# Pair attention on one core: one product for four pairs through widened queries and values

## The chip, the cores and the metric

One core of a Trainium2 chip runs the whole program. The time is the device time of one execution in microseconds; the reference for it is the median of three executions. A profiled execution is a separate one, and its rows give the durations used below. PE is TensorE, DVE is VectorE, ACT is ScalarE, POOL is GpSimd, SP issues the DMAs; PEld stands for TensorE's weight loads.

## What is computed

The program is a small Perceiver of six stages on a state x of 64 batches, 32 tokens and 128 features (2048 tokens). The change lies in the fifth stage, whose reference is, cut to what matters:

```python
x = x + attn(layernorm(x), Wq, Wk, Wv)        # b, s, d = 64, 32, 128; H = 16, dk = 8

Q = (x @ Wq.T).reshape(H, b, s, dk)           # a plain reshape, K and V the same way
scores = einsum('hbqd,hbkd->hbqk', Q, K)
out = einsum('hbqk,hbkd->hbqd', softmax(scores, -1), V).reshape(b, s, -1)
y = out + x
(y - mean(y, axis=(1, 2))) / sqrt(var(y, axis=(1, 2)) + 1e-5)
```

The reshape doesn't split heads by feature: 32 rows of one "head and batch" are two tokens in a row with their 16 slices of 8 features. So attention runs within pairs of neighbouring tokens: 1024 pairs, each with a 32x32 score matrix and 8 features of depth.

## The kernel before

All is float32. The state lies with features on partitions, [128, 2048]. `perceiver` runs the stages one after the other with a barrier between them; `l1_attention` (from L1345) is the stage in question. Within it each engine has its own program in order, and semaphores tie them together.

Front: mean and variance over features by products with a constant matrix (L1499, L1503), normalised x in `xn`; projections q, k, v in four parts of 512 tokens (`project`, L1509), copied out of PSUM by ScalarE (`keep`, L1591, q and v) and VectorE (k, L1708). A DMA stores each part in DRAM (L1437), another reads it back by head (`by_heads`, L1442): group g (512 tokens) lies on partitions 32g to 32g+32, of which every fourth holds one of the 8 features; the other 24 stay zero, for which GpSimd clears the three tiles first (L1489). The free axis is [16 slices, 512 tokens].

Block loop: eight blocks of 32 pairs in each of the four groups, 128 pairs and 1024 columns a block. GpSimd reorders q into a row per pair (`q_st`, L1494). `scores(i)` on TensorE makes 128 products, each of 32 rows, 32 columns and 32 moving columns, on one of the four diagonal 32x32 tiles of the array; `turns` orders them so that neighbours in time lie in different groups. VectorE's `softmax(i)`: maximum (L1658), subtraction (L1661), then the exponential on ScalarE (L1595), sum (L1663), reciprocal (L1665), product (L1667), transpose of each 32x32 block (L1670). `turn_v` copies and transposes the values of the next block (L1650, L1653). `outputs(i)` makes 128 products of the same form (L1532), and ScalarE's `keep_output` copies the result into `o8` (L1599), which is the q tile. Scores have two PSUM buffers, outputs one. TensorE's order is scores(0), scores(1), outputs(0), scores(2), outputs(1) and so on.

Each two blocks complete 128 tokens of every group, a chunk of 512 tokens: SP stores them (L1470) and reads them back with features on partitions (L1484); VectorE adds the residual (L1680), and sums over 16 batches at a time lead to the centred, scaled result added to x (L1682 to L1698), with TensorE's L1538 and L1543 and ScalarE's L1603, L1608, L1610 in between. The last chunk's chain ends the stage.

Other lines named below: L2746 (products of the fourth stage, 128x128 loads, 32 moving columns), L1863 and L1899 (first stage), L1114 (the router of the sixth stage, 128x128 loads, 8 moving columns).

Of the kernel before, what the change touches and what calls it, by code (L numbers as in the profile page):

```python
# [6 lines left out]
P = 128  # L7
B, S, D = 64, 32, 128
TOK = B * S
# [3 lines left out]
F32 = mybir.dt.float32  # L13
# [1330 lines left out]

def l1_attention(nc, x_in, consts, dram):  # L1345
# [3 lines left out]
    with ExitStack() as ctx:  # L1349
        def sb(name, shape, dt=F32):  # L1350
# [4 lines left out]
        ones, eps5 = consts["mean"], consts["eps5"]  # L1355
        ps = ctx.enter_context(nc.psum_tensor("t_ps", [P, 8 * BANK], F32))
        scratch = [nc.dram_tensor(f"t_scratch{i}", (P, TOK), F32, kind="Internal").ap() for i in range(4)]
# [4 lines left out]
        by_head = [sb(n + "8", [P, HEADS, GTOK]) for n in "qkv"]  # L1362
        q_st = sb("qs", [P, 2, BCOL])
        v_st = sb("vs", [P, BCOL])
        v_rows = sb("v_rows", [P, 2, BCOL])
# [4 lines left out]
        o8, o_t, square = by_head[0], tmp, q_t  # L1370
# [4 lines left out]
        w_loaded, cleared = sem("w_loaded"), sem("cleared")  # L1375
        projected, kept, spread = ([sem(what + n) for n in "qkv"] for what in ("projected_", "kept_", "spread_"))
        stored = [[sem(f"stored_{n}{p}") for p in range(4)] for n in "qkv"]
        q_staged, v_staged, v_turned, scored, maxed, shifted, exped, summed, inverted, scaled, p_turned, attended, o_kept = (
            sem(n) for n in ("q_staged", "v_staged", "v_turned", "scored", "maxed", "shifted", "exped", "summed",
                             "inverted", "scaled", "p_turned", "attended", "o_kept"))  # L1380
        o_stored = sem("o_stored")
# [13 lines left out]

        out_ps = ps[:, 4 * BANK:4 * BANK + BCOL]
# [5 lines left out]
        def heads_of(ap, i):  # L1402

            return ap[:, :, i * 2 * BPAIRS:(i + 1) * 2 * BPAIRS].rearrange("p j (n t) -> p n j t", t=2)
# [4 lines left out]
        def turns():  # L1409

            for s in range(BPAIRS):
                for g in range(GROUPS):
                    yield g, (s + g * BPAIRS // GROUPS) % BPAIRS

        def chunk(ap, c):

            return ap[:, :].rearrange("p (g t) -> p g t", g=GROUPS)[:, :, c * P:(c + 1) * P]

        def packed(ap, c):

            return ap[:, of(c)].rearrange("p (g t) -> p g t", g=GROUPS)

        def rows_in(g):
            return slice(32 * g, 32 * (g + 1), ROW_STEP)

        def in_scratch(i, g, first, last):

            return scratch[i].rearrange("(j c) t -> c j t", c=DH)[:, :, g * GTOK + first:g * GTOK + last]

        with nc.Block() as block:  # L1430
            @block.sync
            def _(sp):
                sp.dma_start(wqkv[:, :, :], dram["attn1"]).then_inc(w_loaded, 16)

                def store(i, p):
                    sp.wait_ge(kept[i], p + 1)
                    sp.dma_start(scratch[i][:, of(p)], qkv_t[i][:, of(p)]).then_inc(stored[i][p], 16)  # L1437

                def by_heads(i, p):
                    sp.wait_ge(stored[i][p], 16)  # L1440
                    sp.wait_ge(cleared, i + 1)
                    sp.dma_start(by_head[i][rows_in(p), :, :], in_scratch(i, p, 0, GTOK)).then_inc(spread[i], 16)  # L1442

                store(0, 0)
                store(0, 1)
                store(1, 0)
                by_heads(0, 0)
                store(0, 2)
                store(1, 1)
                by_heads(0, 1)  # L1450
                by_heads(1, 0)
                store(0, 3)
                store(1, 2)
                by_heads(0, 2)
                by_heads(1, 1)
                store(1, 3)
                by_heads(0, 3)
                store(2, 0)
                by_heads(1, 2)
                store(2, 1)  # L1460
                by_heads(1, 3)
                store(2, 2)
                by_heads(2, 0)
                store(2, 3)
                for p in range(1, 4):
                    by_heads(2, p)

                def store_output(first, last):
                    for g in range(GROUPS):
                        sp.dma_start(in_scratch(3, g, first, last), o8[rows_in(g), :, first:last]).then_inc(o_stored, 16)  # L1470

                stores = 0
                for c in range(CHUNKS):
                    if c < CHUNKS - 1:
                        sp.wait_ge(o_kept, 2 * c + 2)
                        store_output(c * P, (c + 1) * P)
                        stores += GROUPS
                    else:
                        for h in range(2):
                            sp.wait_ge(o_kept, 2 * c + 1 + h)  # L1480
                            store_output(c * P + h * (P // 2), c * P + (h + 1) * (P // 2))
                            stores += GROUPS
                    sp.wait_ge(o_stored, 16 * stores)
                    sp.dma_start(packed(o_t, c), chunk(scratch[3], c)).then_inc(o_loaded[c], 16)  # L1484
# [12 lines left out]
            def _(pe):  # L1497
# [7 lines left out]
                def project(i, p):  # L1505
# [3 lines left out]
                    nc.tensor.matmul(bank(4 + p if i == 1 else p), wqkv[:, i, :], xn[:, of(p)],  # L1509
                                     start=True, stop=True).then_inc(projected[i], 1)  # L1510
# [1578 lines left out]
```

## Time and profile before

| | |
|---|---|
| median of 3 executions | 2837.02 us (2836.5 to 2841.46) |
| profiled execution | 2837.81 us, span 2835.7 us |
| mean granted TensorE clock | 0.925 |
| PE / PEld busy | 2469.1 us (87%) / 1394.8 us (49%) |
| DVE / ACT / POOL busy | 2181.6 us (77%) / 1854.4 us (65%) / 841.8 us (30%) |
| pair attention | about 2410 to 2576 us of the span |
| L1522 + L1532 (its products), recorded busy | 32.6 + 32.8 us |

Busy is the time in which an engine has at least one instruction recorded; matmuls are pipelined, so the mean length of one (237 ns for L1522) is latency and not its share of the time: that is read from how many lie in a stretch. Granted clock 1.00 is 2.4 GHz, 0.50 is 1.2 GHz. "Issue" is time in which an engine waited for nothing that the profile shows. The shares are over all six stages; what a change in one is worth is read from that stage's own windows.

### The profile page before, as it was taken

To read this page: it belongs to the slowest core of one execution; us is meant where nothing else is said; L and a number is where in the kernel's file an instruction comes from. 1 tells how busy PE (TensorE), PEld (TensorE's weight loads), DVE (VectorE), ACT (ScalarE), POOL (GpSimd) and SP (SyncE) were. 2 spreads that over 40 slices of the span, in tenths; PEclk is the share of its full clock that TensorE was granted. 3 is DMA by queue.
4 is the path that set the end of the run, shared out by engine and by line. 5 is a ranking of instruction groups with operands and counts; after the bars stand their busy time and mean duration, and the time that the engine had idled before them with its cause. 6 is when DMAs were issued, how large, how long until landed. Compare 5 with 4: busy or idle time off the path is not lost. (4 is left out here: it accounts for less than half of the span.)

```text
span 2835.7 us, 35494 instructions
## 1 busy us (share of the span) xinstructions
PE 2469.1 (87%) x12324; PEld 1394.8 (49%) x12350; DVE 2181.6 (77%) x2846; ACT 1854.4 (65%) x2597; POOL 841.8 (30%) x470
## 2 busy tenths in 40 slices
PE   6799999998799999999999999998446887556997
PEld 3466666663344444444444444443124776354775
DVE  5687777772999999999999999996557776465554
ACT  5465555554799888888889988886425664214443
POOL 0121211111444444444444444443001000301554
PEclk9999999999999999999999999999657999656999
DMA  1000000002000000000000000000000110200221
GB/s 69 12 19 16 17 18 16 15 1 82 0 0 0 38 0 38 0 37 0 38 0 23 14 0 38 0 0 0 12 21 15 37 37 15 94 27 25 76 69 38
DMA packets 26069, 68.11 MB, mean 24 GB/s; under 512 B 3192, under 2 KB 15288, under 8 KB 24632
## 3 DMA queue, kind: packets, MB, share of 16 engines
q1 hardware_dynamic: 25632, 64.13, 6.6%
q8 instruction: 81, 1.33, 0.2%
q10 hardware_dynamic: 288, 2.10, 0.2%
q14 instruction: 68, 0.56, 0.1%
HBM read 60.91 MB, written 5.31 MB: 23 GB/s over the span
## 5 line engine op out<-in xcount | busy, mean ns | idle before, releaser
L251 PE MATMUL a_ps<-a_x,a_w 128*128 128x512 f32 x1536 | 695.9, 598 | 25.8 <-DVE a_kf L599 13.2
L251 PEld LDWEIGHTS a_ps<-a_x,a_w 128*128 128x128 f32 x1536 | 291.6, 191 | 405.5 <-issue 368.0
L774 POOL TENSOR_TENSOR a_den<-a_qf,a_ksum 128x1024 f32<-128x1024 f32 x128 | 271.0, 2117 | 512.4 <-DVE a_qf L592 475.8
L777 POOL TENSOR_TENSOR a_num<-a_qf,a_kvsum 128x1024 f32<-128x1024 f32 x128 | 294.8, 2303 | 185.6 <-DVE a_kvsum L617 185.6
L2425 DVE TENSOR_REDUCE x_rn<-x_sqk 128x8 f32<-128x512 f32 x256 | 174.3, 682 | 106.4 <-ACT x_sqk L2349 102.3
L2349 ACT ACTIVATE x_sqk<-x_b_k 128x512 f32<-128x512 f32 x256 | 153.1, 598 | 157.2 <-PE x_b_k L2261 150.9
L262 PE MATMUL a_ps<-a_att,a_w 128*128 128x512 f32 x480 | 215.8, 592 | 0.0
L592 DVE SCALAR_TENSOR_TENSOR a_qf<-a_eq,a_qf 128x1024 f32<-128x1024 f32 x128 | 195.4, 1527 | 1.7
L2242 POOL TENSOR_TENSOR x_kn<-x_craw,x_w 128x256 f32<-128x256 f32 x64 | 46.9, 734 | 503.8 <-DVE x_craw L2414 482.2
L445 ACT ACTIVATE a_den<-a_den,consts 128x1024 f32<-128x1024 f32 x128 | 147.0, 1149 | 55.9 <-POOL a_den L774 55.9
L599 DVE SCALAR_TENSOR_TENSOR a_kf<-a_ek,a_ps 128x1024 f32<-128x1024 f32 x128 | 155.6, 1215 | 30.2 <-ACT a_ps L441 22.8
L611 DVE SCALAR_TENSOR_TENSOR a_ek<-a_ps,a_w,a_kf 128x1024 f32<-128x1024 f32 x128 | 163.2, 1275 | 9.9 <-PE a_ps L251 9.8
L440 ACT ACTIVATE a_ek<-a_ps,a_w 128x1024 f32<-128x1024 f32 x128 | 142.2, 1111 | 36.5 <-PE a_ps L251 30.5
L2261 PE MATMUL x_b_k<-x_wk_hi,x_kt_hi 128*128 128x512 f32 x256 | 160.2, 626 | 4.7 <-DVE x_kt_lo L2420 4.7
L624 DVE SCALAR_TENSOR_TENSOR a_att<-a_num,a_den 128x1024 f32<-128x1024 f32 x128 | 155.7, 1217 | 5.4 <-ACT a_den L447 4.3
L433 ACT ACTIVATE a_eq<-a_ps,a_w 128x1024 f32<-128x1024 f32 x128 | 142.1, 1110 | 24.4 <-PE a_ps L251 16.7
L605 DVE TENSOR_REDUCE a_ksum<-a_kf 128x32 f32<-128x1024 f32 x128 | 155.2, 1212 | 1.1
L617 DVE TENSOR_REDUCE a_kvsum<-a_ek 128x32 f32<-128x1024 f32 x128 | 155.3, 1213 | 0.6
L1229 POOL TENSOR_TENSOR m_hid_lo<-m_hid,m_hid_hi 128x1024 fp32r<-128x1024 f32 (+1 forms) x48 | 118.1, 2462 | 118.1 <-ACT m_hid_hi L1197 117.7
L262 PEld LDWEIGHTS a_ps<-a_att,a_w 128*128 128x128 f32 x480 | 91.2, 190 | 114.8 <-issue 114.8
L434 ACT ACTIVATE a_qf<-a_ps,a_w 128x1024 f32<-128x1024 f32 x128 | 142.4, 1113 | 0.0
L2275 PE MATMUL x_b_y<-x_sc,x_kn 128*128 128x512 f32 x256 | 140.4, 633 | 0.5 <-DVE x_sc L2435 0.5
(398 smaller groups left out, 5307.9 us busy)
## 6 DMA issues: line engine op xcount, KB each, us to landing
a_w<-layers SPq DMA_DIRECT2D x8, 2577.0 KB, 9.4
x_craw<-ctx SPq DMA_DIRECT2D x32, 256.0 KB, 2.7
y_cx<-ctx_t SPq DMA_DIRECT2D x16, 512.0 KB, 3.6
m_wb<-m_scratch SPq DMA_DIRECT2D x16, 512.0 KB, 3.8
m_w<-experts SPq DMA_DIRECT2D x8, 544.0 KB, 4.9
x_w<-xattn_w ACTq DMA_DIRECT2D x1, 1536.0 KB, 9.4
x_all<-x_t SPq DMA_DIRECT2D x4, 256.0 KB, 9.3
t_scratch<-t_q_t SPq DMA_DIRECT2D x4, 256.0 KB, 3.7
```

The costliest lines, as they stand in the source:

```text
L251: last = nc.tensor.matmul(bank(tile, j), col(par, part * HK + u * P, P), x[:, t0:t0 + BANK], start=True, stop=True)
L262: last = nc.tensor.matmul(bank(tile_t, j), col(par, C_WO + c * D, D), bank(att[:, half, c, :], j), start=(c == 0), stop=(c == CH - 1))
L592: nc.vector.scalar_tensor_tensor(out=qf[:, b, :], in0=eq[:, b, :], scalar=1.0, in1=qf[:, b, :], op0=ALU.add, op1=ALU.add).then_inc(q_feat, 1)
L599: nc.vector.scalar_tensor_tensor(out=kf[:, b, :], in0=ek[:, b, :], scalar=1.0, in1=tile_k[:, :], op0=ALU.min, op1=ALU.add).then_inc(k_feat, 1)
L605: nc.vector.tensor_reduce(ksum[:, b, :], by_batch(kf[:, b, :]), AX_X, ALU.add).then_inc(k_summed, 1)
L611: nc.vector.scalar_tensor_tensor(out=ek[:, b, :], in0=tile_v[:, :], scalar=bias(par, C_BV + u), in1=kf[:, b, :], op0=ALU.add, op1=ALU.mult ...
L617: nc.vector.tensor_reduce(kvsum[:, b, :], by_batch(ek[:, b, :]), AX_X, ALU.add).then_inc(kv_summed, 1)
L624: nc.vector.scalar_tensor_tensor(out=att[:, half, c, :], in0=num[:, b, :], scalar=1.0, in1=den[:, b, :], op0=ALU.mult, op1=ALU.mult).then_ ...
L774: nc.gpsimd.tensor_tensor(by_batch(den[:, b, :]), by_batch(qf[:, b, :]), bcast(ksum[:, b, :], S), ALU.mult).then_inc(d_ready, 1)
L777: nc.gpsimd.tensor_tensor(by_batch(num[:, b, :]), by_batch(qf[:, b, :]), bcast(kvsum[:, b, :], S), ALU.mult).then_inc(n_ready, 1)
L2261: last = nc.tensor.matmul(b_k[n % 2][:, :], a[:, b % 4, t], k[:, f], start=(p == 0), stop=(p == 2))
L2425: nc.vector.tensor_reduce(rn[:, b % 4, 8 * c:8 * c + 8], sqk[:, n % 2, :].rearrange("p (h d) -> p h d", d=XDH), AX_X, ALU.add).then_inc(n_ ...
```

## The change

The queries lie on all 32 partitions of a group: feature c of token part p (four parts of 128 tokens) on partition 4c + p. A group of 512 tokens is now worked through in two blocks of 64 tokens of each part (block i: group i // 2, half i % 2), so that a block still has 128 pairs and 1024 columns. For each of the block's 32 places, four pairs (one of each part) share the same 32 partitions. `q_st` becomes four copies of the queries side by side, in copy p all partitions but those of part p multiplied by zero (`wide`; mask `own_row`): three copies by ScalarE (`widen`), the fourth by GpSimd. One product with 32 rows, 128 columns and 32 moving columns then gives the scores of four pairs on 128 partitions, 32 products a block. The values are turned once for all groups (`turn_v`, 2048 columns); `own_values(g)` on ScalarE spreads group g's into `v_own` by four masked copies of 512 elements, so that one product with 128 rows, 32 columns and 32 moving columns gives four pairs' outputs. The probabilities' softmax and transpose stay as they are. There is a tile `o8` of its own, no memsets, one store a block and one load a group (now plain 512 tokens), loads and stores go through new DRAM layouts (runs of 512 B and 2 KB; the output's stores 256 B), and each group's q and k have their own semaphores. The projections' order changes: v's part p follows q's closely, in the same bank. The constants get the two masks.

```diff
 
 
+NPART = 4
+PTOK = GTOK // NPART
+NPAIR = PTOK // 2
+NB = BCOL // PAIR_ROWS
...
+        O_SCRATCH = 2
         xn = sb("xn", [P, TOK])
         tmp = sb("tmp", [P, TOK])
         wqkv = sb("wqkv", [P, 3, P])
...
+        q_st = sb("qs", [P, 2, NPART * NB * PAIR_ROWS])
+        v_st = sb("vs", [P, NPAIR * PAIR_ROWS])
+        v_rows = sb("v_rows", [P, NPAIR * PAIR_ROWS])
+        v_own = sb("v_own", [P, 2, NPAIR * PAIR_ROWS])
         prob = sb("prob", [P, BCOL])
         prob_t = sb("prob_t", [P, 2, BCOL])
-        red = sb("red", [P, BPAIRS])
+        red = sb("red", [P, NB])
...
             sem(n) for n in ("mean_ready", "centred", "squared", "var_ready", "logged", "rstd_ready", "normed"))
-        w_loaded, cleared = sem("w_loaded"), sem("cleared")
...
+        def wide(i, p):
+
+            return q_st[group_rows(i // 2), i % 2, :].rearrange("r (n a j t) -> r n a j t", a=NPART, j=HEADS, t=2)[:, :, p, :, :]
+
+        def group_rows(g):
+            return slice(32 * g, 32 * (g + 1))
+
+        def by_row(i, g):
+
+            return scratch[i][g].rearrange("j r t -> r j t")
+
+        def by_feature(i, g):
+
+            return scratch[i][g].rearrange("j (c p) t -> (j c) (p t)", c=DH)
+
+        def values_by_row(p):
+            return v_scratch[:, :, p, :].rearrange("j r t -> r j t")
+
+        def values_by_feature(g):
+            return v_scratch.rearrange("j (c g) p t -> (j c) g (p t)", c=DH)[:, g, :]
 
...
+                    sp.dma_start(values_by_feature(p) if i == 2 else by_feature(i, p), qkv_t[i][:, of(p)]).then_inc(stored[i][p], 16)
+
+                def by_heads(i, g):
+                    sp.wait_ge(stored[i][g], 16)
+                    sp.dma_start(by_head[i][group_rows(g), :, :], by_row(i, g)).then_inc(spread[i][g], 16)
+
+                def values_by_part(p):
+                    for g in range(GROUPS):
+                        sp.wait_ge(stored[2][g], 16)
+                    sp.dma_start(v8[group_rows(p), :, :], values_by_row(p)).then_inc(v_spread, 16)
 
...
                 store(0, 0)
+                store(1, 0)
+                store(2, 0)
+                store(2, 1)
+                by_heads(0, 0)
+                by_heads(1, 0)
+                store(2, 2)
...
+                store(1, 1)
+                for p in range(NPART):
+                    values_by_part(p)
+                by_heads(0, 1)
+                by_heads(1, 1)
...
+                for g in range(2, GROUPS):
+                    by_heads(0, g)
+                    by_heads(1, g)
+
+                for i in range(BLOCKS):
+                    g, h = i // 2, i % 2
+                    t = slice(h * (PTOK // 2), (h + 1) * (PTOK // 2))
+                    sp.wait_ge(o_kept, i + 1)
+                    sp.dma_start(by_row(O_SCRATCH, g)[:, :, t], o8[group_rows(g), :, t]).then_inc(o_stored[g], 16)
+                    if h == 1:
+                        sp.wait_ge(o_stored[g], 32)
+                        sp.dma_start(o_t[:, of(g)], by_feature(O_SCRATCH, g)).then_inc(o_loaded[g], 16)
 
             @block.gpsimd
             def _(pool):
-                for t in by_head:
-                    nc.gpsimd.memset(t[:, :, :], 0.0).then_inc(cleared, 1)
                 for i in range(BLOCKS):
-                    if i == 0:
-                        pool.wait_ge(spread[0], 16 * GROUPS)
-                    wait_past(pool, scored, i - 1)
-                    nc.gpsimd.tensor_copy(rows_of(q_st[:, i % 2, :]), heads_of(by_head[0], i)).then_inc(q_staged, 1)
+                    if i % 2 == 0:
+                        pool.wait_ge(spread[0][i // 2], 16)
+                    r, p = group_rows(i // 2), NPART - 1
+                    nc.gpsimd.tensor_scalar(wide(i, p), by_pair(q8[r, :, :], i % 2 * NB, (i % 2 + 1) * NB), own_row[r, p:p + 1], None,
+                                            ALU.mult).then_inc(q_masked, 1)
 
...
                 def scores(i):
-                    pe.wait_ge(q_staged, i + 1)
-                    if i == 0:
-                        pe.wait_ge(spread[1], 16 * GROUPS)
+                    g, h = i // 2, i % 2
+                    pe.wait_ge(q_widened, (NPART - 1) * (i + 1))
+                    pe.wait_ge(q_masked, i + 1)
+                    pe.wait_ge(spread[1][g], 16)
                     wait_past(pe, shifted, i - 1)
...
-                    out = scores_of(i)
-                    for g, n in turns():
-                        c = slice(n * PAIR_ROWS, (n + 1) * PAIR_ROWS)
-                        r = slice(32 * g, 32 * g + 32)
-                        t = 2 * (i * BPAIRS + n)
-                        last = nc.tensor.matmul(out[r, c], q_st[r, i % 2, c], by_head[1][r, :, t:t + 2], start=True, stop=True)
+                    out, r = scores_of(i), group_rows(g)
+                    for n in range(NB):
+                        t = 2 * (h * NB + n)
+                        last = nc.tensor.matmul(out[:, n * PAIR_ROWS:(n + 1) * PAIR_ROWS], q_st[r, h, n * P:(n + 1) * P], k8[r, :, t:t + 2],
+                                                start=True, stop=True)
                     last.then_inc(scored, 1)
 
                 def outputs(i):
-                    pe.wait_ge(v_turned, i + 1)
+                    g, h = i // 2, i % 2
+                    pe.wait_ge(v_masked, NPART * (g + 1))
                     pe.wait_ge(p_turned, i + 1)
                     wait_past(pe, o_kept, i)
-                    for g, n in turns():
+                    for n in range(NB):
                         c = slice(n * PAIR_ROWS, (n + 1) * PAIR_ROWS)
-                        r = slice(32 * g, 32 * g + 32)
-                        last = nc.tensor.matmul(out_ps[r, c], v_rows[r, i % 2, c], prob_t[r, i % 2, c], start=True, stop=True)
+                        v = slice((h * NB + n) * PAIR_ROWS, (h * NB + n + 1) * PAIR_ROWS)
+                        last = nc.tensor.matmul(out_ps[group_rows(g), c], v_own[:, g % 2, v], prob_t[:, i % 2, c], start=True, stop=True)
                     last.then_inc(attended, 1)
...
                 project(0, 0)
+                project(1, 0)
+                project(2, 0)
                 project(0, 1)
-                project(1, 0)
-                project(0, 2)
+                project(2, 1)
                 project(1, 1)
-                project(0, 3)
-                project(1, 2)
-                project(1, 3)
-                for p in range(4):
+                for p in range(2, 4):
+                    project(0, p)
                     project(2, p)
+                    project(1, p)
...
+                def widen(i):
+                    if i % 2 == 0:
+                        act.wait_ge(spread[0][i // 2], 16)
+                    r = group_rows(i // 2)
+                    for p in range(NPART - 1):
+                        nc.scalar.activation(wide(i, p), by_pair(q8[r, :, :], i % 2 * NB, (i % 2 + 1) * NB), ACT.Copy,
+                                             scale=own_row[r, p:p + 1]).then_inc(q_widened, 1)
+
+                def own_values(g):
+                    act.wait_ge(v_turned, 1)
+                    wait_past(act, attended, 2 * (g - 1))
+                    turned = v_rows[:, :].rearrange("k (n c g) -> k n c g", g=GROUPS, c=DH)
+                    dst = v_own[:, g % 2, :].rearrange("k (n c a) -> k n c a", a=NPART, c=DH)
+                    for p in range(NPART):
+                        nc.scalar.activation(dst[:, :, :, p], turned[:, :, :, g], ACT.Copy, scale=own_group[:, p:p + 1]).then_inc(v_masked, 1)
+
                 def keep_output(i):
+                    r = group_rows(i // 2)
                     act.wait_ge(attended, i + 1)
-                    nc.scalar.activation(heads_of(o8, i), rows_of(out_ps), ACT.Copy).then_inc(o_kept, 1)
+                    nc.scalar.activation(by_pair(o8[r, :, :], i % 2 * NB, (i % 2 + 1) * NB), rows_of(out_ps[r, :]), ACT.Copy).then_inc(o_kept, 1)
 
                 def squares(c):
...
                 exponentials(0)
-                for i in range(1, 5):
-                    exponentials(i)
-                    keep_output(i - 1)
+                widen(2)
+                exponentials(1)
+                own_values(0)
+                keep_output(0)
+                exponentials(2)
+                widen(3)
+                keep_output(1)
+                own_values(1)
+                exponentials(3)
+                widen(4)
+                keep_output(2)
+                exponentials(4)
...
                 keep_output(4)
...
+                own_values(3)
...
-                def turn_v(i):
-                    if i == 0:
-                        dve.wait_ge(spread[2], 16 * GROUPS)
-                    wait_past(dve, v_turned, i)
-                    nc.vector.tensor_copy(rows_of(v_st[:, :]), heads_of(by_head[2], i)).then_inc(v_staged, 1)
-                    dve.wait_ge(v_staged, i + 1)
-                    wait_past(dve, attended, i - 1)
-                    nc.vector.transpose(v_rows[:, i % 2, :], v_st[:, :]).then_inc(v_turned, 1)
+                def turn_v():
+                    dve.wait_ge(v_spread, 16 * NPART)
+                    nc.vector.tensor_copy(rows_of(v_st[:, :]), by_pair(v8, 0, NPAIR)).then_inc(v_staged, 1)
+                    dve.wait_ge(v_staged, 1)
...
+                    if i == 0:
+                        turn_v()
                     if i == 3:
                         add_residual(0)
                     if i == 4:
...
+    for a in range(4):
+        c[:, 264 + a] = np.arange(P) % 4 == a
+        c[:, 268 + a] = np.arange(P) // 32 == a
```

## Rows read from the trace of the kernel before

**Rows 1.** Windows of this stage: us, then each engine's busy time, PEclk, DMA.
```profile
core 0: us, PE busy (x) PEld busy (x) DVE busy (x) ACT busy (x) POOL busy (x), PEclk, DMA share, GB/s
2428.80:2441.50 12.70, 0.00 (x0) 0.00 (x0) 0.00 (x0) 0.00 (x0) 3.97 (x3) 0.68 0.66 247
2441.50:2560.70 119.20, 63.97 (x4103) 59.60 (x4103) 74.16 (x78) 17.77 (x19) 6.34 (x6) 0.50 0.10 29
```
**Rows 2.** Groups of instructions by form, 2404 to 2592 us: busy, mean, idle before.
```profile
line engine op names shapes xcount | busy us, mean ns | idle before us <-releasers
L1532 PE MATMUL t_ps<-t_prob_t,t_v_rows 32*32 32x32 f32 x2048 | 32.8, 237 | 29.3 <-issue 23.9 <-DVE t_prob_t L1670 4.0 <-ACT t_q L1599 1.3
L1522 PE MATMUL t_ps<-t_k,t_qs 32*32 32x32 f32 x2048 | 32.6, 237 | 39.3 <-issue 25.9 <-DMA t_k<-t_scratch 13.4
...
L1653 DVE STREAM_TRANSPOSE t_v_rows<-t_vs 128x1024 f32<-128x1024 f32 x8 | 10.0, 1245 | 0.3
...
L1599 ACT ACTIVATE t_q<-t_ps 128x1024 f32<-128x1024 f32 x8 | 8.6, 1076 | 30.7 <-PE t_ps L1532 30.7
L1595 ACT ACTIVATE t_prob<-t_prob 128x1024 f32<-128x1024 f32 x8 | 8.5, 1056 | 72.1 <-DVE t_prob L1661 72.1
L1494 POOL COPY t_qs<-t_q 128x1024 f32<-128x1024 f32 x8 | 8.4, 1055 | 78.2 <-PE t_ps L1522 71.4 <-DMA t_q<-t_scratch 6.9
...
L1650 DVE COPY t_vs<-t_v 128x1024 f32<-128x1024 f32 x8 | 5.3, 659 | 23.0 <-DMA t_v<-t_scratch 23.0
```
**Rows 3.** Timeline of blocks 3 and 7: start, length, then idle time before.
```profile
2481.53 1.93 PE L1522 MATMUL t_ps<-t_k,t_qs 32*32 32x32 f32 x128 [1.96 <-issue]
...
2486.84 1.22 DVE L1658 TENSOR_REDUCE t_red<-t_ps 128x32 f32<-128x1024 f32 x1 [6.17 <-PE t_ps L1522]
...
2489.36 1.06 ACT L1595 ACTIVATE t_prob<-t_prob 128x1024 f32<-128x1024 f32 x1 [9.34 <-DVE t_prob L1661]
...
2493.35 1.25 DVE L1670 STREAM_TRANSPOSE t_prob_t<-t_prob 128x1024 f32<-128x1024 f32 x1
...
2545.62 1.23 DVE L1658 TENSOR_REDUCE t_red<-t_ps 128x32 f32<-128x1024 f32 x1 [3.41 <-PE t_ps L1522]
```
**Rows 4.** Timeline of the front of the stage: memset, last copy, first product.
```profile
2423.82 6.92 POOL L1489 MEMSET t_v<- 128x8192 f32 x1
...
2428.18 0.60 ACT L1591 ACTIVATE t_v_t<-t_ps 128x512 f32<-128x512 f32 x1 [0.26 <-PE t_ps L1509]
...
2441.55 2.67 PE L1522 MATMUL t_ps<-t_k,t_qs 32*32 32x32 f32 x183 [13.41 <-DMA t_k<-t_scratch]
```
**Rows 5.** Timeline, weight loads alone: the first load after a wait, four forms.
```profile
2399.98 0.19 PEld L2746 LDWEIGHTS y_ps<-y_qt,y_kvm 128*128 128x128 f32 x1 [1.17 <-DVE y_qk L2956]
...
87.22 0.11 PEld L1899 LDWEIGHTS x_pa<-x_wvo,x_kn_cols 128*32 128x32 f32 x1 [0.17 <-issue]
...
2501.70 0.29 PEld L1538 LDWEIGHTS t_ps<-t_sums,consts 128*128 128x128 f32 x1
...
2441.52 0.12 PEld L1522 LDWEIGHTS t_ps<-t_k,t_qs 32*32 32x32 f32 x1 [14.21 <-issue]
```
**Rows 6.** Timeline of three streams of loads; window of the first one's clock.
```profile
2591.05 3.11 PEld L1114 LDWEIGHTS m_ps<-m_router,m_xn 128*128 128x128 f32 x14
...
2399.98 0.97 PEld L2746 LDWEIGHTS y_ps<-y_qt,y_kvm 128*128 128x128 f32 x8 [1.17 <-DVE y_qk L2956]
...
24.15 1.86 PEld L1863 LDWEIGHTS x_pa<-x_w 64*128 64x128 f32 x16 [1.60 <-issue]
...
2591.00:2594.80 3.80, 3.80 (x20) 3.80 (x19) 1.63 (x2) 1.26 (x3) 0.00 (x0) 0.50 0.00 0
```
**Rows 7.** The page's DMA issues: count, KB each, median us to landing.
```profile
t_scratch<-t_q_t SPq DMA_DIRECT2D x4, 256.0 KB, 3.7
```
**Rows 8.** Timeline of the end of the stage, from the last output copy on.
```profile
2560.78 1.04 ACT L1599 ACTIVATE t_q<-t_ps 128x1024 f32<-128x1024 f32 x1 [6.48 <-PE t_ps L1532]
...
2567.85 0.69 DVE L1698 TENSOR_TENSOR x_all<-x_all,t_tmp 128x512 f32<-128x512 f32 x1
2568.92 0.69 DVE L1680 TENSOR_TENSOR t_tmp<-t_tmp,t_xn 128x512 f32<-128x512 f32 x1 [0.38 <-DMA t_tmp<-t_scratch]
...
2575.30 0.69 DVE L1698 TENSOR_TENSOR x_all<-x_all,t_tmp 128x512 f32<-128x512 f32 x1
```

More of the change, by code:

```diff
@@ L1353, in l1_attention @@
         sem = ctx.enter_context(semaphores(nc, "t_"))
-        ones, eps5 = consts["mean"], consts["eps5"]
+        ones, eps5, own_row, own_group = consts["mean"], consts["eps5"], consts["own_row"], consts["own_group"]
         ps = ctx.enter_context(nc.psum_tensor("t_ps", [P, 8 * BANK], F32))
-        scratch = [nc.dram_tensor(f"t_scratch{i}", (P, TOK), F32, kind="Internal").ap() for i in range(4)]
+        scratch = [[nc.dram_tensor(f"t_scratch{i}{g}", (HEADS, DH * NPART, PTOK), F32, kind="Internal").ap() for g in range(GROUPS)]
+                   for i in range(3)]
+        v_scratch = nc.dram_tensor("t_v_scratch", (HEADS, DH * GROUPS, NPART, PTOK), F32, kind="Internal").ap()
+        O_SCRATCH = 2
         xn = sb("xn", [P, TOK])
@@ L1394, in scores_of, with project_bank @@
             return ps[:, i % 2 * BCOL:(i % 2 + 1) * BCOL]
+        def project_bank(i, p):
+            return bank(4 + p if i == 1 else p)
         out_ps = ps[:, 4 * BANK:4 * BANK + BCOL]
@@ L1400, in pairs, with by_pair @@
             return ap.rearrange("p (n r) -> p n r", r=PAIR_ROWS)
-        def heads_of(ap, i):
-            return ap[:, :, i * 2 * BPAIRS:(i + 1) * 2 * BPAIRS].rearrange("p j (n t) -> p n j t", t=2)
+        def by_pair(ap, first, last):
+            return ap[:, :, 2 * first:2 * last].rearrange("p j (n t) -> p n j t", t=2)
         def rows_of(ap):
             return ap.rearrange("p (n j t) -> p n j t", j=HEADS, t=2)
[L1409 to L1428, printed above, removed]
+        def wide(i, p):
[10 more added lines that the diff above has]
+            return v_scratch.rearrange("j (c g) p t -> (j c) g (p t)", c=DH)[:, g, :]
         with nc.Block() as block:
@@ L1452, in _ @@
                 store(0, 3)
-                store(1, 2)
-                by_heads(0, 2)
-                by_heads(1, 1)
                 store(1, 3)
[L1457 to L1484, printed above, removed]
+                for g in range(2, GROUPS):
+                    by_heads(0, g)
+                    by_heads(1, g)
@@ L1508, in project @@
                         pe.wait_ge(kept[0], p + 1)
-                    nc.tensor.matmul(bank(4 + p if i == 1 else p), wqkv[:, i, :], xn[:, of(p)],
+                    nc.tensor.matmul(project_bank(i, p), wqkv[:, i, :], xn[:, of(p)],
                                      start=True, stop=True).then_inc(projected[i], 1)
                 def scores(i):
-                    pe.wait_ge(q_staged, i + 1)
-                    if i == 0:
-                        pe.wait_ge(spread[1], 16 * GROUPS)
+                    g, h = i // 2, i % 2
@@ L1590, in keep @@
                     act.wait_ge(projected[i], p + 1)
-                    nc.scalar.activation(qkv_t[i][:, of(p)], bank(p), ACT.Copy).then_inc(kept[i], 1)
+                    nc.scalar.activation(qkv_t[i][:, of(p)], project_bank(i, p), ACT.Copy).then_inc(kept[i], 1)
                 def exponentials(i):
@@ L1620, in _ @@
                     nc.scalar.activation(tmp[:, of(p)], tmp[:, of(p)], ACT.Exp, scale=-0.5).then_inc(rstd_ready, 1)
-                for i in (0, 2):
-                    for p in range(4):
-                        keep(i, p)
-                exponentials(0)
-                for i in range(1, 5):
-                    exponentials(i)
-                    keep_output(i - 1)
+                for p in range(4):
+                    keep(0, p)
+                    keep(2, p)
+                widen(0)
+                widen(1)
+                exponentials(0)
+                widen(2)
[10 more added lines that the diff above has]
+                exponentials(4)
+                widen(5)
+                keep_output(3)
+                own_values(2)
                 squares(0)
                 exponentials(5)
+                widen(6)
                 keep_output(4)
@@ L1632, in _ @@
                 exponentials(6)
+                widen(7)
                 keep_output(5)
+                own_values(3)
                 squares(1)
@@ L1697, in finish @@
                     dve.wait_ge(y_normed, c + 1)
-                    nc.vector.tensor_tensor(chunk(x_in, c), chunk(x_in, c), packed(o_t, c), ALU.add).then_inc(out_done, 1)
+                    nc.vector.tensor_tensor(x_in[:, of(c)], x_in[:, of(c)], o_t[:, of(c)], ALU.add).then_inc(out_done, 1)
                 for p in range(4):
@@ L3029, in consts_of @@
     return {"mean": c[:, 0:128], "ident": c[:, 128:256], "eps5": c[:, 256:257], "eps6": c[:, 257:258],
-            "ln256": c[:, 258:259], "eps10": c[:, 259:260], "all": c[:, :]}
+            "ln256": c[:, 258:259], "eps10": c[:, 259:260], "own_row": c[:, 264:268],
+            "own_group": c[:, 268:272], "all": c[:, :]}
 def pack_layers(a):
```

37 lines of the change are left out of this document (14 added, 23 removed).

## The prediction

> **What bounds the kernel now.** The span is a row of stages separated by barriers, and the change touches one of them, the pair attention, which runs from about 2410 to 2576.0 us. So I read by stage: first the windows over the block loop, then the groups of this stage, then one block in the timeline. In the loop (2441.5 to 2560.7, 119.2 us) TensorE is recorded busy 64.0 us and VectorE 74.2 us, and neither looks full; the granted clock is 0.50 all through, so TensorE is at 1.2 GHz [rows 1]. The reader is to see that the busy shares mislead. Each block has 128 score products and 128 output products, and the trace has 2048 matmul records for the 1024 products of either kind, so a product is two passes [rows 2]. A batch of 128 passes takes 1.93 us and then the engine stands 1.96 us on "issue" [rows 3]: it waits for its own instructions. Two batches for scores and two for outputs make 4 x 3.9 = 15.6 us at most; the start of the softmax moves from 2486.84 to 2545.62 in four blocks, 14.7 us each [rows 3]. The softmax itself, from the first reduction at 2486.84 to the end of the transpose (2493.35 + 1.25), is 7.76 us, so VectorE waits for TensorE in each block. The bound is the number of TensorE instructions.
>
> **What is removed.** A block now has 32 + 32 products instead of 128 + 128: 64 passes for scores and 64 for outputs. The issue stalls end; at the present pace (128 passes in 3.9 us) 64 would need 2.0 us, and the work on the array will be longer than that. The memsets go: the third ended at 2423.82 + 6.92 = 2430.7, 10.8 us before the first product, which waited for the load of k [rows 4], so this is worth nothing by itself. Seven of eight value turns leave VectorE, where it waits anyway.
>
> **What a score product costs now.** This is the term that decides. Each product loads 128 columns of widened queries (32 rows deep) and streams only 32 columns of keys. The stage has only loads of 32x32, so I take the load from elsewhere, by the first load after a wait, which has nothing in front of it. At the high clock 128x128 takes 0.19 us and 128x32 takes 0.11 [rows 5]: 96 columns more cost 0.08, 0.83 ns a column. At the low clock 128x128 takes 0.29 and 32x32 takes 0.12 [rows 5]: 0.17 for 96 columns, which is the doubled rate (0.16) although the second is 32 rows deep. So the load goes by columns, the rows give nothing back, and 128 columns cost 107 ns at the high and 213 ns at the low clock.
> Streams confirm it: 14 loads of 128 columns before products with 8 moving columns take 3.11 us at clock 0.50, (3.11 - 0.33)/13 = 0.214 us each, and at the high clock 8 loads before 32 moving columns take 0.97, (0.97 - 0.19)/7 = 0.111 [rows 6]. The 32 moving columns are hidden under the next load, on the same rows; so too with 64 rows, 16 in 1.86 us, 0.111 each, where load and stream are both 128 columns [rows 6].
> Now the clock. In the loop it is low already. Of the new stream the nearest row is the one of the router: TensorE busy 3.80 of 3.80 us with loads of 128 columns and short moving sides, and the clock stays at 0.50 [rows 6]. I take the low clock. Scores of a block: 63 x 0.213 + 0.07 + 0.37 for the last product = 13.9 us, against about 7.8 now. Bounds: 0.111 a pass (high clock, 7.3 us) and 0.267 (load and stream one after the other, 17.3 us).
>
> **What an output product costs.** 128 rows, 32 columns to load, 32 to stream: 53 ns each at the low clock. Today four row groups work side by side and 128 passes take 1.93 us, (1.93 - 0.24)/127 x 4 = 53 ns for each group [rows 2, 3], so load and stream overlap: 64 x 0.053 + 0.2 = 3.6 us; bounds 1.9 (high clock) and 7.0 (one after the other).
>
> **What is added on ScalarE, and who waits.** widen(i) is three activations of 1024 elements a partition, 1.06 us each by the exponential and the strided output copy [rows 2]: 3.24 us a block; own_values(g) is four of 512 elements, 4 x (0.60 + 0.05) = 2.6 us [rows 4]. They are 32 partitions wide, which I don't count as cheaper. From block 3 on the order on ScalarE is exponentials(i), widen(i+1). The exponential needs scores(i), and scores(i+1) needs widen(i+1). So the two score buffers no longer let TensorE run ahead; each block is a ring: scores 13.9, then to VectorE and through reduction and subtraction 0.09 + 1.26 + 1.26, exponential to its end 1.06, widening 3.27, back to TensorE 0.07: 13.9 + 7.0 = 20.9 us. (2489.36 - 2486.84 = 2.52 is the start of the exponential after the start of the softmax [rows 3].) Outputs (3.6), the output copy and own_values lie beside it, as does the rest of the softmax; GpSimd's masking of the fourth part (1.06 us by its copy of q [rows 2]) waits for its load only.
>
> **The sum.** Start: today the last copy of the projections ends at 2428.8 [rows 4]. In the new order each projection of v waits for the copy of q of its part in the same bank, 0.6 + 0.2 us four times, and the last copy ends at about 2431.8. The q and k loads of group 0 are issued by 2427 and stores of this size land in 3.7 us [rows 7], so they are there. widen(0) ends at 2435.1; the first scores start at 2435.2, 6.3 us earlier than today's 2441.55 [rows 4]. Bounds for this start: 2433 and 2438.
> First blocks: scores(0) and scores(1) end at 2463.0. VectorE has finished softmax(0) and the one turn of all values (twice 0.66 + 1.25 [rows 2], 3.85 us) by 2460.8, under cover of scores(1). exponentials(1) ends 3.6 later, own_values(0), queued behind it, 2.6 after that, and outputs(0) waits for both: 3.6, then scores(2) 13.9. The softmax of block 2 starts at 2486.7.
> Blocks 3 to 7: 5 x 20.9 = 104.5, so softmax(7) starts at 2591.2, against 2545.62.
> End: softmax 7.8, outputs(7) 3.6, copy 1.1. Today the copy ends at 2561.82, the last chunk's first addition is at 2568.92 and the stage ends at 2575.99 [rows 8]. The new store is one issue instead of four, but VectorE finishes chunk 2 only at 2568.54 [rows 8], a chain behind the same copy, so 13.8 of today's 14.2 us stay. The stage ends at 2591.2 + 26.3 = 2617.5, which is 41.5 us later. The clock fell today some 5 us after the last projection (mean 0.68 over 2428.8 to 2441.5 [rows 1]: 4.6 us at 1.00); the new scores begin 3 us after it, so some 16 passes run at the high level and give back 1.7 us. 39.8 more.
> The profiled execution took 2837.81 us (span 2835.7), 0.8 over the median of 2837.02. 2837.8 + 39.8 = 2877.6, predicted as 2878. Its own range: start +-3, ring +-0.4 five times, outputs serial twice (+7), high clock through scores(0) (-7): 2866 to 2890.
>
> **Rivals.**
> Fast, high clock (faster): the longer products keep TensorE at 2.4 GHz. With 7.3 and 1.9 us: 2435.2 + 7.3 + 11.6 (now VectorE's softmax(0) and turn) + 3.6 + 2.6 + 1.9 + 7.3 = 2469.5; + 5 x 14.3 = 2541.0; + 24.6 = 2565.6, 10.4 us earlier, 2827. For it: TensorE would be busy for 17.5 of 20.9 us in the forecast, where now it is 64.0 of 119.2 [rows 1]. Against it: the router's rows. The point from which the sign turns is a score stage of 8.3 us, that is 0.130 us a pass, since the time is 2517.9 + 7 x stage while the stage is under 11.6.
> Fast, cheap load (faster): 128 columns load in 107 ns at the low clock too when only 32 rows are filled: scores 7.1, 2470.8 + 5 x 14.1 + 26.3 = 2567.6, 8.4 earlier, 2829. Against it: 0.12 for 32x32 fits the column rate without any discount.
> The Trainium skill, page "TensorE: Matmul & The Clock Gate", section "LDWEIGHTS (loading the stationary operand)", gives columns / 1.2 ns whatever the rows, an estimate of 107 ns; by it the sum would be this rival's. The trace has that for fp32 only at the high clock and twice it (0.214) at the low one.
> Serial (slower still): load and stream don't overlap within one group of 32 rows: passes of 0.267 and 0.107, stages of 17.3 and 7.0: 2435.2 + 3 x 17.3 + 6.2 + 7.0 = 2500.3, + 5 x 24.3 + 29.7 = 2651.5, 75.5 later, 2913. Against it: the 64-row stream at 0.111.
> The same page, section "Part 3: Packing small matmuls — row/col tiling", says that a load overlaps running products only where the row group differs; by that rule this rival is the forecast. The trace disagrees for the full array and for 64 rows, and has no 32-row tile with one group alone.
> Issue-bound as the change supposes (products nearly free) would need passes of about 30 ns; the load rows exclude it.
>
> **How the numbers follow.** Forecast 0.79; high clock 0.07; cheap load 0.06; serial 0.06; something near no change 0.02. So slower 0.85, faster 0.13, within 0.2% 0.02; 0.2% is 5.7 us, about what a measurement of this kernel can tell from none. The range takes the forecast's own, 2 us of slack below, and the serial case above: 2864 to 2914, 0.82.
>
> **What would show it.** In the profile after: score products 64 records a block with loads about 0.33 us long and 0.213 apart; clock 0.50 over the loop; softmax starts 20.9 us apart, VectorE's first reduction waiting for TensorE some 13 us each time; TensorE waiting for ScalarE's widening about 3.4 us a block; no long waits on issue. Wrong if the passes are 0.11 apart, or if the blocks come at under 15 us.

## The result, and the profile after

| | before | after |
|---|---|---|
| median (range), us | 2837.71 (2836.5 to 2841.46) | 2878.54 (2877.65 to 2880.17) |
| profiled span, us | 2835.7 | 2878.4 |
| pair attention, first mean product to last addition, us | 165.9 | 204.1 |
| before it / behind it in the span, us | 2410.1 / 259.7 | 2412.1 / 262.2 |

The ratio is 1.0142 (95% interval 1.0125 to 1.0160): slower by 40.8 us, where 2878 was predicted. The spans differ by 42.7 us: 38.3 in the changed stage, 1.9 ahead of it and 2.5 behind it. These two lie in work that the change does not touch: over the ten kernels profiled in this study the stage begins between 2407.8 and 2412.1 us, with the same work ahead, and what follows it takes 257.6 to 262.8.

The groups of the block loop in the kernel after (columns as in [rows 2], 2437.7 to 2602.4 us):
```profile
L1529 PE MATMUL t_ps<-t_k,t_qs 32*128 32x32 f32 x512 | 105.5, 384 | 19.3 <-ACT t_qs L1611 19.3
...
L1541 PE MATMUL t_ps<-t_prob_t,t_v_own 128*32 128x32 f32 x512 | 28.4, 239 | 12.4 <-ACT t_v_own L1620 8.1 <-DVE t_prob_t L1710 4.3
...
L1611 ACT ACTIVATE t_qs<-t_q,consts 32x1024 f32<-32x1024 f32 x21 | 23.1, 1160 | 0.1
L1620 ACT ACTIVATE t_v_own<-t_v_rows,consts 128x512 f32<-128x512 f32 x16 | 18.0, 1213 | 0.1
L1501 POOL TENSOR_SCALAR t_qs<-t_q,consts 32x1024 f32<-32x1024 f32 x6 | 17.5, 2922 | 8.7 <-DMA t_q<-t_scratch 8.3
...
L1698 DVE TENSOR_REDUCE t_red<-t_ps 128x32 f32<-128x1024 f32 x8 | 9.8, 1225 | 90.7 <-PE t_ps L1529 90.7
```
TensorE has a quarter of the passes (512 where [rows 2] had 2048) and the wait "issue", 23.9 and 25.9 us there, is gone; yet the score passes are busy 105.5 us instead of 32.6, and the reduction that opens the softmax waits 90.7 us for them, in all eight blocks.

One full block of the timeline, after (start, length, idle time before):
```profile
2507.69 1.22 DVE L1698 TENSOR_REDUCE t_red<-t_ps 128x32 f32<-128x1024 f32 x1 [13.10 <-PE t_ps L1529]
...
2510.21 1.06 ACT L1604 ACTIVATE t_prob<-t_prob 128x1024 f32<-128x1024 f32 x1 [10.86 <-DVE t_prob L1701]
2511.29 3.30 ACT L1611 ACTIVATE t_qs<-t_q,consts 32x1024 f32<-32x1024 f32 x3
...
2514.64 13.86 PE L1529 MATMUL t_ps<-t_k,t_qs 32*128 32x32 f32 x64 [3.77 <-ACT t_qs L1611]
...
2528.53 1.23 DVE L1698 TENSOR_REDUCE t_red<-t_ps 128x32 f32<-128x1024 f32 x1 [11.80 <-PE t_ps L1529]
```
This is the ring: reduction at 2507.69, exponential, three widenings behind it, 64 passes (32 products) in 13.86 us, and the next reduction 20.84 us after the last one. In [rows 3] the softmax started every 14.7 us.

The clock, in windows of the same kernel (columns as in [rows 1]):
```profile
2437.70:2602.40 164.70, 135.93 (x1034) 134.40 (x1034) 63.16 (x64) 59.00 (x58) 17.53 (x6) 0.54 0.15 33
...
2528.50:2549.40 20.90, 18.00 (x132) 17.77 (x133) 7.26 (x9) 10.38 (x10) 0.00 (x0) 0.50 0.07 20
```
Low nearly throughout, though TensorE is busy for 135.9 of 164.7 us.

### The profile page after: what moved, and what is told of

Its sections match the earlier page's. It is cut to its first block and busy times, and to the rows that moved or that the text cites. A ratio compares the mean times of both kernels' runs of the same rounds, so it can differ in the third digit from the quotient of the medians.

```text
span 2878.4 us, 29362 instructions
## 1 busy us (share of the span) xinstructions
PE 2545.3 (88%) x9252; PEld 1472.2 (51%) x9278; DVE 2169.9 (75%) x2832; ACT 1898.1 (66%) x2637; POOL 836.3 (29%) x467
```

## The experiments

Eight kernels, each beside the kernel before. Where a row of the trace answers, it decides; whole times add what moves outside the stage. The kernel before took 2837.74 us beside four of them (the widening moved, the half load, the longer moving side, the outputs alone) and 2841.78 beside the other four, on another chip; each ratio is to the one beside it.

**The ring.** Here ScalarE widens the queries of block i+1 ahead of exponentials(i), from block 2 on.
```diff
-exponentials(2)
 widen(3)
+exponentials(2)
 keep_output(1)
```
(and so for widen(4) to widen(7))

> The changed kernel with one thing moved on ScalarE: widen(i+1) stands ahead of exponentials(i) from block 2 on. Theory (a ring through ScalarE): the score stage of the next block no longer waits for exponential and widening, so the softmax starts come at TensorE's own pace, 64 score passes of 0.213 plus 64 output passes of 0.053, about 17.2 us apart instead of 20.8; five such steps give 18 us, about 2860 us, and the waits of TensorE for the widening (19.3 us in all) nearly vanish. Rival (TensorE's work alone sets the pace, the waits are filled by it anyway): no change, 2878 us.

Measured 2855.39 us, ratio 1.0062 (1.0040 to 1.0083). The start of a block, as above:
```profile
2503.07 3.62 PE L1541 MATMUL t_ps<-t_prob_t,t_v_own 128*32 128x32 f32 x64
2503.18 1.23 DVE L1698 TENSOR_REDUCE t_red<-t_ps 128x32 f32<-128x1024 f32 x1 [9.59 <-PE t_ps L1529]
...
2506.62 13.86 PE L1529 MATMUL t_ps<-t_k,t_qs 32*128 32x32 f32 x64
...
2520.52 1.23 DVE L1698 TENSOR_REDUCE t_red<-t_ps 128x32 f32<-128x1024 f32 x1 [8.29 <-PE t_ps L1529]
```
Steps of 17.34 us: the products of the next block begin straight behind the outputs, and 3.62 + 13.86 = 17.48 of TensorE's own work is now the step. The widening behind the exponential was worth 3.5 us a block. The profiled stage takes 187.2 us instead of 204.1, 17 us less; the median is 23 us below that of the changed kernel, and what exceeds 17 lies outside the stage or between executions (this profile is of the slowest of five, 2861.75 us). Even without it the kernel stays slower than before: its score stage alone nearly fills an old block.

**The price by columns.** Each score product loads 64 of the 128 weight columns; the scores of the other two pairs of each product are not computed.
```diff
-nc.tensor.matmul(out[:, n * PAIR_ROWS:(n + 1) * PAIR_ROWS], q_st[r, h, n * P:(n + 1) * P], k8[r, :, t:t + 2],
+nc.tensor.matmul(out[0:64, n * PAIR_ROWS:(n + 1) * PAIR_ROWS], q_st[r, h, n * P:n * P + 64], k8[r, :, t:t + 2],
```


> The changed kernel with the load of each score product cut from 128 to 64 columns: two of the four pairs are left out (their rows keep old values), so its output is not the reference's. Theory (a score pass costs its weight columns, 1.67 ns each at the low clock): passes of 0.107, score stages of 7.1 instead of 13.9 us, blocks about 14.0 us apart instead of 20.8; 34 us over five blocks and about 10 before them, about 2834 us. Rival (a pass of this form has a fixed price whatever it loads): 2878 us.

Measured 2826.90 us, ratio 0.9964 (0.9952 to 0.9977).
```profile
2493.87 7.03 PE L1529 MATMUL t_ps<-t_k,t_qs 32*64 32x32 f32 x64 [3.43 <-ACT t_qs L1611]
...
2500.94 1.23 DVE L1698 TENSOR_REDUCE t_red<-t_ps 128x32 f32<-128x1024 f32 x1 [4.97 <-PE t_ps L1529]
```
Half the columns take half the time (7.03 against 13.86 us for 64 passes), at the same count of instructions and the same 32 moving columns. Steps fell to 14.0, and some passes ran at the higher clock (two of the stages take 6.40 and 6.49 us). So neither the count nor the moving side sets this stage.

**Longer moving side.** The changed kernel with 128 moving columns for each score product (the keys four times over; each column of the result is written again by its own product later).
```diff
-last = nc.tensor.matmul(out[:, n * PAIR_ROWS:(n + 1) * PAIR_ROWS], q_st[r, h, n * P:(n + 1) * P], k8[r, :, t:t + 2],
+m = min(4, 16 - n % 16)
+moving = k8[r, :, t:t + 2].unsqueeze(1).broadcast_to([32, m, HEADS, 2])
+last = nc.tensor.matmul(out[:, n * PAIR_ROWS:(n + m) * PAIR_ROWS], q_st[r, h, n * P:(n + 1) * P], moving,
```

> The changed kernel, each score product with up to 128 moving columns instead of 32: the same 32 key columns repeated four times, the surplus columns of the result being overwritten by the next products, so the result stays the same and TensorE does up to four times the streaming. Theory (load-bound at the low clock; the clock is low because the array mostly stands while weights load): the pass stays at 0.213 us at the low clock, since 128 columns load as long as 128 stream, but the granted clock rises to 1.00 in the score stages and the pass falls to about 0.11; blocks 14 to 15 us apart, about 2840 us. Rival A (clock stays at 0.50): unchanged within a few us, 2878 to 2882. Rival B (load and stream don't overlap on one group of 32 rows): passes of 0.43, over 2950 us.

Measured 2877.61 us, ratio 1.0138 (1.0112 to 1.0164).
```profile
2437.00:2600.00 163.00, 132.17 (x1016) 130.63 (x1014) 64.72 (x68) 56.55 (x56) 17.63 (x6) 0.55 0.13 30
...
2510.36 13.86 PE L1531 MATMUL t_ps<-t_k,t_qs 32*128 32x128 f32 x64 [3.65 <-ACT t_qs L1613]
```
Four times the streaming cost nothing: 13.86 us again, clock 0.55. I had expected the clock to rise, and was wrong. What it does show is that within one group of 32 rows a load of 128 columns and a stream of 128 columns lie fully side by side, which excludes the serial rival: by it this kernel's 64 passes would take some 27 us (an estimate, 0.213 us for the load and as much for the stream) and the changed kernel's 17.3. The Trainium skill, page "TensorE: Matmul & The Clock Gate", section "Part 3: Packing small matmuls — row/col tiling", has two statements: a load is pulled ahead where the row group differs or where it goes to the background weight buffer, and, below, it overlaps running products only where the row group differs. This trace disagrees with the second.

**All rows.** Two kernels whose score products use all 128 rows (rows of other groups' queries and keys are added in, so their scores are not the reference's), one with 32, one with 128 moving columns. Both wait for all loads of k and for cleared query buffers, and their first product starts 16.6 us late, counted from the start of the stage.
```diff
-nc.tensor.matmul(out[:, n * PAIR_ROWS:(n + 1) * PAIR_ROWS], q_st[r, h, n * P:(n + 1) * P], k8[r, :, t:t + 2],
+moving = k8[:, :, t:t + 2].unsqueeze(1).broadcast_to([P, m, HEADS, 2])
+nc.tensor.matmul(out[:, n * PAIR_ROWS:(n + m) * PAIR_ROWS], q_st[:, h, n * P:(n + 1) * P], moving,
```
(m is 1 in the first, and as in the kernel above in the second)

> The kernel before this one with 32 moving columns again: score products on all 128 rows (not the reference's scores), 128 weight columns, 32 moving. If rows fill time in a load, a pass takes longer than the 0.213 us of 32 rows; if a load goes by columns alone, 64 passes take 13.9 us at clock 0.50 as before, steps of 20.8, and the time is that of the changed kernel and the late start, about 2883. If full rows raise the clock, 7.3 us and 2835.

> The changed kernel with every score product on all 128 rows (the queries and keys of the other three groups are streamed too, so the scores are not the reference's, where those rows aren't zero) and 128 moving columns. It waits for all loads of k and for two cleared query buffers first, so the first block starts up to 6 us later. Rival A with a filled array (the clock would rise, if the array had more to do): 64 passes in 7.3 us, softmax steps of 14.3 us, about 2835 with the late start. My theory after the run with 128 moving columns (that stream stayed at 0.50; the router's stream with full loads too): 13.9 us, steps of 20.8, about 2883. I take the second with 0.6.

Measured 2891.53 and 2867.68 us (one time each, beside 2841.78 for the kernel before on that chip). The first, with 32 moving columns, then the second, with 128, and two of its windows:
```profile
2508.61 13.86 PE L1538 MATMUL t_ps<-t_k,t_qs 128*128 128x32 f32 x64 [3.80 <-ACT t_qs L1622]
```
```profile
2484.44 7.33 PE L1538 MATMUL t_ps<-t_k,t_qs 128*128 128x128 f32 x64
...
2498.77 10.06 PE L1538 MATMUL t_ps<-t_k,t_qs 128*128 128x128 f32 x64 [4.84 <-ACT t_qs L1622]
...
2498.80:2504.00 5.20, 5.20 (x24) 5.20 (x25) 0.77 (x1) 5.17 (x5) 0.00 (x0) 0.50 0.27 75
2504.00:2508.80 4.80, 4.80 (x43) 4.76 (x42) 0.00 (x0) 0.36 (x1) 0.00 (x0) 0.95 0.00 0
```
Rows are free in a load: 128 rows take the 13.86 us of 32; this kernel's stage is 17.9 us longer than the changed one's, nearly all of it the late start. With all rows and 128 moving columns the granted clock did rise during the stream, from 0.50 to 0.95, and the 64 passes took 10.06 us, or 7.33 where the clock was 1.00 from the start: the figure the prediction gave for that rival (7.3). I had taken the low clock for this kernel with 0.6, and missed; its steps, 17.06 us, lie between both expectations and are the ring again, 10.06 + 7.0. So the high-clock rival named a real mechanism, and the change doesn't reach it. Neither the rows alone (the first of these kernels) nor the moving columns alone (the kernel above) did.

**own_values earlier.** own_values(0) ahead of exponentials(1):
```diff
-exponentials(1)
 own_values(0)
+exponentials(1)
```


> The changed kernel with own_values(0) ahead of exponentials(1) on ScalarE. In the changed kernel the four value activations stood behind that exponential and ended at 2472.5 us; outputs(0) waited 8.1 us for them. Theory (that wait is on the path through blocks 0 to 2, and my sum had it too short): they now run from about 2461.7, end at 2466.2, before exponentials(1) is due at 2467.0; outputs(0) starts 6.2 us earlier, and the time falls by 4 to 6 us, to about 2873. The steps of blocks 3 to 7 stay at 20.8 us. If it is the score products of block 2 alone that set the start of softmax 2, nothing moves: 2878.

Measured 2870.58 us, ratio 1.0100 (1.0083 to 1.0117).
```profile
2459.44 4.50 ACT L1620 ACTIVATE t_v_own<-t_v_rows,consts 128x512 f32<-128x512 f32 x4 [4.39 <-DVE t_v_rows L1693]
...
2463.99 3.42 PE L1541 MATMUL t_ps<-t_prob_t,t_v_own 128*32 128x32 f32 x64 [2.23 <-ACT t_v_own L1620]
```
outputs(0) starts 54.5 us into the stage instead of 60.4, and the stage takes 198.9 us instead of 204.1: 5.2 less, with unchanged steps of 20.84. The span fell by 12.2; the other 7 lie outside the stage (2.6 ahead of it, 4.4 behind).

**Outputs alone by four.** The kernel before, with its scores unchanged (32x32, four groups side by side). v of group p goes to partitions 32p + 4c + p instead of 32p + 4c, and one product of 128 rows serves four pairs.
```diff
-sp.dma_start(by_head[i][rows_in(p), :, :], in_scratch(i, p, 0, GTOK)).then_inc(spread[i], 16)
+rows = slice(33 * p, 32 * (p + 1), ROW_STEP) if i == 2 else rows_in(p)
+sp.dma_start(by_head[i][rows, :, :], in_scratch(i, p, 0, GTOK)).then_inc(spread[i], 16)
...
-for g, n in turns():
+for n in range(BPAIRS):
     c = slice(n * PAIR_ROWS, (n + 1) * PAIR_ROWS)
-    last = nc.tensor.matmul(out_ps[r, c], v_rows[r, i % 2, c], prob_t[r, i % 2, c], start=True, stop=True)
+    last = nc.tensor.matmul(out_ps[0:32, c], v_rows[:, i % 2, c], prob_t[:, i % 2, c], start=True, stop=True)
```
The output copy and the stores of o8 follow: 32 partitions, one group on every fourth of them.

> The kernel before, with only the outputs made by one product for four pairs: v of group g goes to the partitions 32g + 4c + g instead of 32g + 4c, so that after the transpose the values of a group already stand in columns that are zero for the other groups, and one product with 128 rows, 32 columns and 32 moving columns gives four pairs' outputs; no masking, scores as before. Theory (before is bound by the number of TensorE instructions): output stage 3.6 instead of 7.8 us, softmax starts about 11.3 us apart instead of 14.7 (VectorE needs 9.8), some 24 us over seven steps and 3 at the end, about 2811 us. Rival (VectorE and the semaphore chain set the pace as soon as TensorE gives way): over 13 us apart, 2825 us or more.

Measured 2813.36 us, ratio 0.9918 (0.9890 to 0.9945): faster than both kernels by 24 and 65 us; it leaves nothing out.
```profile
L1532 PE MATMUL t_ps<-t_prob_t,t_v_rows 128*32 128x32 f32 x512 | 28.2, 237 | 12.1 <-DVE t_prob_t L1670 10.2 <-issue 1.9
...
L1523 PE MATMUL t_ps<-t_k,t_qs 32*32 32x32 f32 x2048 | 26.8, 215 | 34.7 <-issue 20.5 <-DMA t_k<-t_scratch 14.1
...
L1658 DVE TENSOR_REDUCE t_red<-t_ps 128x32 f32<-128x1024 f32 x8 | 9.6, 1200 | 0.0
```
```profile
2467.10 3.62 PE L1532 MATMUL t_ps<-t_prob_t,t_v_rows 128*32 128x32 f32 x64
...
2449.40:2468.40 19.00, 10.39 (x485) 9.77 (x475) 16.41 (x17) 3.08 (x3) 2.15 (x2) 0.59 0.02 4
```
The outputs wait 1.9 us on issue instead of 23.9 [rows 2], and the softmax's first reduction no longer waits for anything. The softmax starts 9.5 to 11.6 us apart (14.7 before). The granted clock was higher too, 0.65 over 2441 to 2534 us where [rows 1] had 0.50, and could claim a part of the gain. It is not what shortened the first two steps, 9.49 us each: the clock was 0.59 there, and the output passes took 3.60 and 3.62 us, their length at the low clock. How much of the later steps it gave is open. The reading that the kernel before is bound by its count of instructions holds, and this half of the change removes it at no cost in loads: four pairs fill 32 output columns, which are the same 32 weight columns as one pair before.

**What bounds that kernel.** The same with the value staging copy moved from VectorE to ScalarE, behind each exponential.
```diff
+def stage_v(i):
+    wait_past(act, v_turned, i)
+    nc.scalar.activation(rows_of(v_st[:, :]), heads_of(by_head[2], i), ACT.Copy).then_inc(v_staged, 1)
...
 exponentials(i)
+stage_v(i + 1)
 keep_output(i - 1)
```


> The kernel with outputs by four (2813.4 us) with the value staging copy moved from VectorE to ScalarE. In that kernel VectorE no longer waited ahead of a softmax: a block took it 7.7 us of softmax and 1.9 to 2.0 of turning the values, 9.5 in all. Theory V (VectorE is its bound): each of seven blocks loses the copy, 0.65 to 0.75 us, so 2808.3, softmax starts 8.8 us apart in the first blocks. Theory T (TensorE stands right behind: 256 score passes in two batches of 3.8 us and 64 output passes in 1.9 to 3.6 make 9.5 to 11 us): the steps stay at 9.5 and more, and the time falls by 1.5 us at most, to 2812 or above.

Measured 2810.22 us, ratio 0.9887 (0.9871 to 0.9904).
```profile
2469.85 1.18 DVE L1665 TENSOR_REDUCE t_red<-t_ps 128x32 f32<-128x1024 f32 x1
...
2478.61 1.18 DVE L1665 TENSOR_REDUCE t_red<-t_ps 128x32 f32<-128x1024 f32 x1
```
Steps of 8.76 us where they were 9.49, and the stage takes 135.8 us instead of 141.2. Theory V holds: VectorE bounds it. In the whole time the gain of 5.4 us can't be told from none: the two kernels ran on different chips, 24.4 and 31.6 us below the kernel before beside each, the intervals of the ratios overlap, and the profiled spans are 2807.6 and 2807.9. The stage began 2.0 us later in this profile, and what follows it took 261.4 us instead of 257.6. There the next stage's router products differ; this kernel first, then the one it was made from:
```profile
2560.97 6.96 PE L1114 MATMUL m_ps<-m_router,m_xn 128*128 128x8 f32 x32 [2.43 <-PEq L105]
```
```profile
2563.49 5.41 PE L1114 MATMUL m_ps<-m_router,m_xn 128*128 128x8 f32 x32 [2.43 <-PEq L105]
```
In all ten profiles the two go together: router 6.96 or 6.97 us with a rest of 261.4 to 262.8 (the kernel after is one of these), 5.79 with 259.7 (before), 5.0 to 5.4 with 257.6 to 258.3. The granted clock goes with it (0.50 over the 6.96 us of the one, 0.66 over the 5.41 of the other). Which edit gives which phase of the clock is open.

## Why the prediction was right

The steps, with the 1.95 us by which this profile's stage started later taken off:

- *Load price.* Forecast 0.213 us a pass at the low clock from loads of another stage; measured 13.86 us for the 64 passes of a block, against 13.9. The half load and the load with all rows confirm both of its premises (columns count, rows don't).
- *Clock.* Low, as the router's row said. Not quite: scores(2) took 10.74 us and scores(7) 12.65. Some of their passes ran at the higher level:
```profile
2476.07 10.74 PE L1529 MATMUL t_ps<-t_k,t_qs 32*128 32x32 f32 x64
...
2476.00:2487.00 11.00, 11.00 (x72) 10.87 (x70) 0.15 (x1) 1.02 (x1) 0.00 (x0) 0.66 0.05 12
```
This gave back 3.2 and 1.2 us that the sum did not have. In scores(0) and scores(1), where it took 1.7 us off, 26.71 us instead of 27.8 give 1.1. That scores(2) follow the outputs straight away does not explain it: with the widening moved, scores(3) to scores(6) do so too and take 13.86 us each. Why these passes got the higher level is open.
- *Front.* Last copy 2432.4 (forecast 2431.8), first scores 2435.8 (2435.2).
- *own_values.* The mis-sized term: 4.50 us for the four, not 2.6. I priced 512 elements by a dense copy (0.60 us each, [rows 4]), but these read and write every fourth element and take 1.21. Neither the source nor the column of factors explains it, since dense activations of 512 elements from SBUF take 0.63 us and with a column of constants 0.67 (L1641 and L1644 of the kernel after); the stride is what is left, and no run varied it alone. outputs(0) started at 2470.6 instead of 2469.2. GpSimd's mask was off by more (2.92 us against 1.06), but lies beside the scores.
- *First blocks.* softmax(2) at 2484.9, forecast 2486.7: +1.4 from the late outputs, -3.2 from the clock.
- *Ring.* 20.84 us (forecast 20.9): 13.86, then 6.95 (7.0) from the reduction to the next product. Moving the widening took out 3.5 of it.
- *End.* 26.3 from softmax(7) to the last addition, forecast 26.3. Stage end 2614.3, forecast 2615.8.
- *The other side.* That the stage grew by 38.3 and not 39.8, and the rest of the span by 4.4, cancels in part: that the whole time agrees better than the steps do (40.8 us against 39.8) is luck.

Of the rivals, "cheap load" fell with the first row: a load takes twice as long at half the clock. The Trainium skill's columns / 1.2 ns ("TensorE: Matmul & The Clock Gate", "LDWEIGHTS (loading the stationary operand)") would give an estimate of 107 ns for 128 columns; the trace has 7.33 us for 64 at clock 1.00, 0.115 each, and 13.86, 0.217 each, at 0.50. Its remark that rows don't matter agrees with the kernel with all rows.

## What to carry to other kernels

Merging small products saves instructions, and here it paid where the merged weights were no wider than before: four pairs in one output product kept 32 weight columns and won 24 us; four pairs in one score product made it 128 columns, and even with the widening moved that kernel is 42 us behind (2855.4 against 2813.4). Count weight columns times products per block, at the clock of that very stage, before counting instructions. A producer queued behind the consumer's follow-up on the same engine (the widening behind the exponential) undoes double buffering, and costs its whole latency in every block.

## What was not expected of the hardware

A load of 128 columns hides a stream of 128 columns even within one group of 32 rows (13.86 us for 64 passes with 32 or with 128 moving columns). An activation of 512 elements a partition took 1.21 us with every fourth element on both sides and 0.60 us dense. GpSimd's multiply by a column took 2.92 us for 32x1024, its copy of 128x1024 1.06 us. And what follows the stage, untouched by the change, took 257.6 to 262.8 us, the longer times with the lower granted clock in its router products: as much as some of the edits here were worth.
